# GRU step of a fused Trainium2 kernel: reset and update gate products laid into one strip of 128 PSUM columns

## What is computed

```python
def cell(h, x):
    gi = x @ W_ih + b_ih
    gh = h @ W_hh + b_hh
    i_r, i_z, i_n = jnp.split(gi, 3, axis=-1)
    h_r, h_z, h_n = jnp.split(gh, 3, axis=-1)
    r = jax.nn.sigmoid(i_r + h_r)
    z = jax.nn.sigmoid(i_z + h_z)
    n = jnp.tanh(i_n + r * h_n)
    h_new = (1.0 - z) * n + z * h
    return (h_new, h_new)
```

## Time and profile before

| | |
|---|---|
| median of 3 runs | 1900.22 us |
| lowest, highest | 1894.44, 1901.37 us |
| span of the profiled execution | 1898.4 us |
| PE, PEld, DVE, ACT, POOL busy | 91%, 61%, 68%, 41%, 16% |
| mean granted clock of PE | 0.992 of full speed |
| matmuls and weight loads | 41087 each |

### The profile page before, as it was taken

One profiled execution on the slowest core, in us unless ns is written; L12 is line 12 of the kernel. 1 busy time (PEld: TensorE's weight loads), 2 busy tenths in 40 slices (PEclk: granted clock), 3 DMA queues, 4 the chain that ended last, 5 costly groups with the idle time before them and its releaser, 6 DMA issues.

```text
span 1898.4 us, 95651 instructions
## 1 busy us (share of the span) xinstructions
PE 1724.2 (91%) x41087; PEld 1165.7 (61%) x41087; DVE 1297.8 (68%) x5788; ACT 779.8 (41%) x2714; POOL 300.4 (16%) x600
## 2 busy tenths in 40 slices
PE   6888888878889999989899999989799999988998
PEld 5777677666556666656566666656566666664444
DVE  6888778887667777767676767667677777764323
ACT  5655566543234343423234444432234444323442
POOL 2222222221211110121211111121211111121001
PEclk8999999999999999999999999999999999999999
DMA  7435444444326667425336677426336666439994
GB/s 259 142 144 195 172 166 170 153 187 137 125 89 193 197 209 220 147 86 147 118 89 196 197 215 212 146 72 169 102 104 203 192 202 192 135 91 372 389 357 147
DMA packets 176689, 334.06 MB, mean 176 GB/s; under 512 B 46448, under 2 KB 46600, under 8 KB 176264
## 3 DMA queue, kind: packets, MB, share of 16 engines
q1 hardware_dynamic: 171144, 311.17, 51.1%
q0 software_dynamic: 5120, 16.78, 2.7%
HBM read 263.10 MB, written 64.78 MB: 173 GB/s over the span
## 4 chain that ended last, share of the span: by engine, by line
PE 66%; DVE 16%; ACT 6%; issue 5%; SPq 3%; DMA 2%; another core or an unknown queue 1%; DVEq 0%; POOL 0%; ACTq 0%
PE bank_g L681 15%; PE bank L967 14%; PE bank_g L686 12%; PE bank_g L697 9%; PE bank L987 7%; DVE xt L1439 5%; DVE na L1445 3%; DVE pre L1441 3%; DVE hs_early L1451 3%; ACT seq_h L1113 3%; ACT rz L1113 3%; PE bank L723 2%; PE bank L963 1%; PE bank L949 1%; PE bank_l L973 1%
## 5 line engine op out<-in xcount | busy, mean ns | idle before, releaser
L1841 POOL COPY hxs<-hs 128x32 f16<-128x32 f16 x512 | 223.8, 437 | 1380.8 <-DVE hs L1459 1380.8
L681 PE MATMUL bank_g<-whh,hs_early 128*32 128x256 f16 x8192 | 319.0, 276 | 123.1 <-DVE hs_early L1451 122.1
L1113 ACT ACTIVATE rz<-pre 128x32 f32<-128x32 f32 x512 | 125.9, 246 | 737.2 <-DVE pre L1441 736.3
L1439 DVE STREAM_TRANSPOSE xt<-bank_g 128x256 f32<-128x256 f32 x512 | 231.0, 451 | 212.8 <-PE bank_g L686 198.8
L681 PEld LDWEIGHTS bank_g<-whh,hs_early 128*32 128x32 f16 x8192 | 171.4, 96 | 318.5 <-DVE hs_early L1451 312.9
L697 PE MATMUL bank_g<-whh,hs 128*32 128x128 f16 x16384 | 327.9, 220 | 10.9 <-issue 10.5
L686 PE MATMUL bank_g<-whh,hs 128*32 128x256 f16 x8192 | 314.6, 274 | 0.1
L967 PE MATMUL bank<-wm,wih 128*128 128x512 f16 x1272 | 309.7, 381 | 3.1 <-issue 2.4
L697 PEld LDWEIGHTS bank_g<-whh,hs 128*32 128x32 f16 x16384 | 259.8, 97 | 15.3 <-issue 12.5
L686 PEld LDWEIGHTS bank_g<-whh,hs 128*32 128x32 f16 x8192 | 204.5, 96 | 22.8 <-DVE hs L1459 3.4
L1113 ACT ACTIVATE seq_h<-na 128x16 f32<-128x16 f32 x512 | 114.9, 224 | 237.5 <-DVE na L1445 237.5
(11 more groups left out here) (245 smaller groups left out, 2063.0 us busy)
## 6 DMA issues: line engine op xcount, KB each, us to landing
wm<-moe_split SPq DMA_DIRECT2D x318, 512.0 KB, 4.5
wm<-in_w_moe SPq DMA_DIRECT2D x32, 768.0 KB, 5.4
moe_split<-wm SPq DMA_DIRECT2D x32, 768.0 KB, 5.1
wih<-x_rows SPq DMA_DIRECT2D x58, 256.0 KB, 4.7
y_rows<-wih SPq DMA_DIRECT2D x58, 256.0 KB, 4.6
whh<-moe_split SPq DMA_DIRECT2D x24, 512.0 KB
gi<-moe_split SPq DMA_DIRECT2D x18, 512.0 KB, 6.6
xr<-in_x SPq DMA_DIRECT2D x16, 512.0 KB, 4.1
```

The source lines that it names most:

```text
L681: mm(out_strip(0, j, 2 * P), early_cols[:, 8 * B * k:8 * B * (k + 1)], strip(whh[:, 1, k, 0:2 * D], j), start=(k == 0), stop=False)
L1113: return nc.scalar.activation(dst, src, func, **kw)
L1439: link(V.transpose(rows, bank_g[0][:, 0:2 * P].rearrange("p (m c) -> p m c", c=32)))
L1841: Q.tensor_copy(hxs[:, par, :, :, :, col].rearrange("p s k b -> p s (k b)"), hs_new).then_inc(S["h_kept"], 1)
```

## The change

The columns of z are no longer laid beside those of r. The state's tile is read two columns further left for z, so that the same state stands in columns 6 and 7 of a group instead of 4 and 5, and z's product comes out in rows 6 and 7 of the same 128 columns that hold r in rows 4 and 5. Two sets (`SETS`), r and z, so share one strip: each matmul has 128 columns, there are twice as many of them, each with its own weight load, and the bank's used part is half as wide. One transposition of 128 columns serves both. The tiles `hs` and `hs_early` get one more group of zeros in front, since z's first piece reads two columns ahead of the first group. `xt` and `pre` are laid out to match, and the access patterns of the input's copy, the reduce and the sigmoid change, with as many elements as before. The n gate is as it was.

```diff
--- before.py
+++ after.py
@@ -32,6 +32,12 @@
 
 
 GROUP = 3
+
+
+
+SETS = 2
+CHUNKS = 2 * K // SETS
+SET_COLS = 2 * D // SETS
 AS, WS = 16.0, 64.0
 PS = AS * WS
 
@@ -219,13 +225,13 @@
         bi = sb("bi", [P, G3], F32)
         bh = sb("bh", [P, G3], F32)
         hh = sb("hh", [P, K * B, 2], F32)
-        hs = sb("hs", [P, K * B, 8], F16)
-        hs_early = sb("hs_early", [P, K * B, 8], F16)
-        xt = sb("xt", [P, 2 * K, 64], F32)
+        hs = sb("hs", [P, 1 + K * B, 8], F16)
+        hs_early = sb("hs_early", [P, 1 + K * B, 8], F16)
+        xt = sb("xt", [P, CHUNKS, 64], F32)
         bias_to = sb("bias_to", [P, 8 * B], F16)
         bias_n = sb("bias_n", [P, D], F16)
         xt_n = sb("xt_n", [P, 4, K * B, GROUP], F32)
-        pre = sb("pre", [P, 2 * K, B], F32)
+        pre = sb("pre", [P, CHUNKS, B, SETS], F32)
         rz = sb("rz", [P, 2 * K * B, GROUP], F32)
         na = sb("na", [P, K * B, GROUP], F32)
         omz = sb("omz", [P, K * B, 2], F32)
@@ -342,16 +348,18 @@
         p_gw = bank_l[1][:, 2 * P:2 * P + B * K * E].rearrange("p (b k e) -> p b k e", b=B, k=K)
         h = hh[:, :, 1:2].rearrange("p (k b) o -> p k (b o)", b=B)
         hs_cols, early_cols = (v[:, :, :].rearrange("p g i -> p (g i)") for v in (hs, hs_early))
-        hs_new = hs[:, :, :].rearrange("p g i -> p i g")[:, 4:6]
+        hs_new = hs[:, 1:].rearrange("p g i -> p i g")[:, 4:6]
         hs_hi, hs_lo = hs_new[:, 0], hs_new[:, 1]
-        early_scan = early_cols.rearrange("p (c s) -> p s c", s=4)[:, 0]
-        early_hi = hs_early[:, :, 4]
-        ext = xt[:, :, 9:16 * B:16]
-        rows = xt[:, :, :].rearrange("p m (c o) -> p m c o", o=2)[:, :, :, 0]
-        terms = xt[:, :, :].rearrange("p m (b i) -> p m b i", i=16)[:, :, :, 8:11]
+        early_scan = early_cols[:, 8:].rearrange("p (c s) -> p s c", s=4)[:, 0]
+        early_hi = hs_early[:, 1:, 4]
+        ext = xt[:, :, :].rearrange("p g (b q i) -> p q g b i", b=B, i=4)[:, SETS:, :, :, 1]
+        rows = xt[:, :, :].rearrange("p g (c o) -> p g c o", o=2)[:, :, :, 0]
+        terms = xt[:, :, :].rearrange("p g (b q i) -> p (g b) q i", b=B, i=4)[:, :, SETS:, 0:3]
         rows_n = xt_n[:, :, :, 0:2].rearrange("p q g s -> p g q s")
         seq_n = xt_n[:, 2]
-        r_new, z_new, n_new = rz[:, :, GROUP - 1:GROUP], rz[:, K * B:, GROUP - 1:GROUP], na[:, :, GROUP - 1:GROUP]
+        pre_sets = pre[:, :, :, :].rearrange("p g b q -> p q (g b)")
+        rz_new = rz[:, :, GROUP - 1:GROUP].rearrange("p (q g) o -> p q (g o)", q=SETS)
+        z_new, n_new = rz[:, K * B:, GROUP - 1:GROUP], na[:, :, GROUP - 1:GROUP]
         pairs = {n: v[:, :, :].rearrange("p a o -> p (a o)") for n, v in
                  (("r", rz[:, 0:K * B]), ("seq_n", seq_n), ("na", na), ("omz", omz), ("seq_h", seq_h), ("hh", hh))}
 
@@ -395,6 +403,14 @@
         def strip(v, j):
 
             return v.rearrange("p (g j c) -> p j g c", j=K, c=32)[:, j]
+
+        def state(v, k, q):
+
+            return v[:, 8 + 8 * B * k - 2 * q:8 + 8 * B * (k + 1) - 2 * q]
+
+        def of_set(w, k, q):
+
+            return whh[:, w, k, q * SET_COLS:(q + 1) * SET_COLS]
 
         def out_strip(i, j, n):
 
@@ -677,14 +693,16 @@
 
                 pe.wait_ge(S["h_hi"], t + 1)
                 for k in range(K):
-                    for j in range(K):
-                        mm(out_strip(0, j, 2 * P), early_cols[:, 8 * B * k:8 * B * (k + 1)],
-                           strip(whh[:, 1, k, 0:2 * D], j), start=(k == 0), stop=False)
+                    for q in range(SETS):
+                        for j in range(K):
+                            mm(out_strip(0, j, SET_COLS // 4), state(early_cols, k, q), strip(of_set(1, k, q), j),
+                               start=(k == 0 and q == 0), stop=False)
                 pe.wait_ge(S["h_ready"], t + 1)
                 for k in range(K):
-                    for j in range(K):
-                        i = mm(out_strip(0, j, 2 * P), hs_cols[:, 8 * B * k:8 * B * (k + 1)],
-                               strip(whh[:, 0, k, 0:2 * D], j), start=False, stop=(k == K - 1))
+                    for q in range(SETS):
+                        for j in range(K):
+                            i = mm(out_strip(0, j, SET_COLS // 4), state(hs_cols, k, q), strip(of_set(0, k, q), j),
+                                   start=False, stop=(k == K - 1 and q == SETS - 1))
                 i.then_inc(S["gates_mm"], 1)
                 if t == 0:
                     pe.wait_ge(S["bias_row"], 1)
@@ -694,7 +712,7 @@
                 for k in range(K):
                     for w in range(2):
                         for j in range(K):
-                            i = mm(out_strip(1, j, P), hs_cols[:, 8 * B * k:8 * B * (k + 1)],
+                            i = mm(out_strip(1, j, P), state(hs_cols, k, 0),
                                    strip(whh[:, w, k, 2 * D:], j), start=False, stop=(k == K - 1 and w == 1))
                 i.then_inc(S["gates_mm"], 1)
 
@@ -1116,14 +1134,13 @@
 
                 act.wait_ge(S["n_pre"], t)
                 now = gi[:, col // TB, :, :, col % TB:col % TB + 1]
-                run(ext.unsqueeze(3), now[:, 0:2 * K], ACT.Copy)
+                run(ext, now[:, 0:2 * K, :, 0].rearrange("p (q g) b -> p q g b", q=SETS), ACT.Copy)
                 run(seq_n[:, :, GROUP - 1:GROUP].rearrange("p (k b) o -> p k b o", b=B), now[:, 2 * K:], ACT.Copy
                     ).then_inc(S["now_in"], 1)
 
             def gru_rz(t):
                 act.wait_ge(S["rz_pre"], t + 1)
-                run(r_new.rearrange("p a o -> p (a o)"), pre[:, :, :].rearrange("p m b -> p (m b)"),
-                    ACT.Sigmoid, scale=1 / PS).then_inc(S["rz_done"], 1)
+                run(rz_new, pre_sets, ACT.Sigmoid, scale=1 / PS).then_inc(S["rz_done"], 1)
 
             def gru_n(t):
                 act.wait_ge(S["n_pre"], t + 1)
@@ -1436,9 +1453,10 @@
                     dve.wait_ge(S["gru_chain"], t * GRU_CHAIN + n[0])
 
                 dve.wait_ge(S["gates_mm"], t * 2 + 1)
-                link(V.transpose(rows, bank_g[0][:, 0:2 * P].rearrange("p (m c) -> p m c", c=32)))
+                link(V.transpose(rows, bank_g[0][:, 0:SET_COLS // 4].rearrange("p (g c) -> p g c", c=32)))
                 dve.wait_ge(S["now_in"], t + 1)
-                V.tensor_reduce(pre[:, :, :], terms, AX, ALU.add).then_inc(S["rz_pre"], 1)
+                V.tensor_reduce(pre[:, :, :, :].rearrange("p g b q -> p (g b) q"), terms, AX, ALU.add
+                                ).then_inc(S["rz_pre"], 1)
                 dve.wait_ge(S["gates_mm"], t * 2 + 2)
                 link(V.transpose(rows_n, bank_g[1][:, 0:P].rearrange("p (g q s) -> p g q s", q=4, s=2)))
                 dve.wait_ge(S["rz_done"], t + 1)
```

## The result

The changed kernel takes 2163.66 us (median of 4 runs, 2152.71 to 2169.81) against 1900.8 us before (4 runs): 1.1395 times as long, with a 95% interval of 1.1354 to 1.1435. The forecast was 1980, its range ended at 2045. The direction and the main cause were as forecast; the loss is 263 us instead of 80.

The account below looks back on a forecast made before the run. The prediction took each GRU step as bound by its 3.13 us loop and PE's list of work: 1900.2 us, less 23 for the shorter loop, plus 103 net for code-fetch stalls, gives 1980; range 1915 to 2045.

Parts of the forecast that it names:

- loop shorter, and stalls that hide in spare time: GRU steps: shorter loop gains 23 us; some 11 us of stalls hide in PE's spare time in the first stretch.
- stalls, less those that were there: PE's chunk borders: 122 us of stalls from late code fetches, less the 8 us already in the run.
- half clock after stalls: PE's clock during or after stalls: the prediction had no such term.
- The loop: GRU step's chain: transposition saves 0.135 us, split product costs 0.022, so 0.113 us shorter where PE has spare time.
- the 14.3 of the sum: First 128 steps: all have the spare time for the shorter loop, a gain of 14.3 us before code stalls.
- The reading of the code stream: PE's instruction fetch: chunks of 256 instructions, two held, the next requested on entering the present; 438 chunks.
- The chunk's duration: PE's 256 instructions last 3.4 us in 74% of positions, some 4.1 us on average else.
- The size of the stall term: Chunk borders: fetches exceed chunk durations by 0.33 or 0.13 us on average; over 438 chunks, 122 us of stalls.
- the bound of 0.3 us: Code fetches: if packets queue behind a denser stream and take 0.3 us longer, 175 us gross, +160 net.
- The hidden fetch: Rival: code is requested early enough, so only the shorter loop's 23 us gain is left: 1877 us; chance 0.13.
- the two that end near zero: Rivals: stalls of 15 to 33 us cancel the gain (1891 to 1910), or dearer slot products (1893); chance 0.08.
- The test that the prediction made on the kernel before: Stall count applied to the kernel before: 310 x 0.04 = 12 us where 8 are seen, so right to a third.

Follow-up runs that it names:

- experiment 1: Kernel before with only its r/z product cut into twice as many matmuls of 128 columns, layout and transposition of 256 kept: 2175.3 us.
- 2: Kernel before with only the late half of its r/z product cut into matmuls of 128 columns, the first product left whole: 1988.06 us.
- 4: Changed kernel with the n product halved (no low half of W_hh), 16 matmuls and 16 weight loads fewer a step, no wait moved: 1961.71 us.
- 5: Changed kernel without the early r/z product and without PE's wait for h_hi, so one wait a step: 1837.24 us.
- experiment 3: Changed kernel without the early r/z product, 32 matmuls and weight loads fewer a step, leaving two PE waits in a row: 1975.98 us.
- experiment 7: Changed kernel with three quarters of the expert weights' columns not loaded in the slots, first two tiles excepted: 1998.58 us, against 2128.09 unchanged.
- 6: Kernel before with one more, already fulfilled, PE wait ahead of each step's first weight load: 1946.09 us.
- experiment 10: Changed kernel run again as it is, on a chip where the kernel before takes 1859.62 us: 2128.09 us.
- experiment 8: Kernel before with VectorE's waits for ACT's results (sigmoid, tanh) written first, ahead of those on its own chain: 1829.42 us against 1859.29.

## Why the prediction was right in kind and wrong in size

The spans differ by 269.6 us, and the 511 steps' intervals account for 270.2 of them. By the steps' records:

| | forecast, us | measured, us |
|---|---|---|
| loop shorter, and stalls that hide in spare time | -23 - 11 = -34 | -35 |
| stalls, less those that were there | 122 - 8 = 114 | 276.6 - 12.8 = 264 |
| half clock after stalls | none | 41 |
| sum | 80 | 270 |

The third row is read from the 44 steps that touch a half clock: they last 88.0 us longer than those of before, their stalls are 46.7 of it. The first row is what is left of the other 467 steps: 182.3 us longer, with 229.9 us of stalls, against before's 12.8. It is a remainder, so that it comes within 1 us of the forecast says less than it seems.

*The loop.* Right. 3.020 us a step in the first stretch (forecast 3.02), 3.127 in the slots (3.12 to 3.13), the transposition 319 ns (316), the product's cost on the loop 0.020 us by experiment 1 (0.02). In the first 128 steps the mean went from 3.189 to 3.748 us, 71.6 in all, while stalls rose by 85.8: the rest is -14.2. That this looks like the 14.3 of the sum is chance: the forecast had another 11 us there, of stalls hidden in spare time, and some 5 us of the rest are half clock. Gain and hidden stalls together are thus about 19 us in this stretch, where 25 were forecast.

*The reading of the code stream.* Right in mechanism: chunks of 256 instructions, one chunk ahead, 438 of them, stalls in hundreds at their borders. Experiments 1, 2 and 4 tie the stalls to the count of instructions, and 1 and 5 clear the rest of the change; experiment 3 shows that the count is not all. The Trainium skill, "Advanced Engine Details and Errata", section "ISA Cache", gives lines of 256 instructions and two of them. The spacing of the stalls, 256, agrees, and so does that in the kernel after no packet starts more than 0.11 us before the chunk ahead of it is entered; nothing here shows more than these two, though the same list gives TensorE 128 KB.

*The chunk's duration.* Right: 3.4 us without its stall was forecast for three of four, the median is 3.39.

*The size of the stall term.* This is the step that failed. The prediction took a fetch as 0.65, 0.86, 1.6 and 2.4 us to the packet's start, plus 2.3, from the kernel before, and got a mean excess of 0.33 us over 3.4 and of 0.13 over 4.1. In the kernel after the start is 1.09, 1.34, 2.05 and 2.96, and from start to use 2.42: the excesses are 0.69 and 0.31, and 438 x (0.74 x 0.69 + 0.26 x 0.31) = 259 us, near the 277 seen. These starts are read from the run itself, so this forecasts nothing, but it shows that the form of the sum held and its input did not. A fetch became 0.6 us longer at the median; the bound of 0.3 us, taken for a denser stream, was too small by half. Two parts of it can be seen. Packets wait in the DMA engines' traffic: with 67 GB/s in the slots instead of 148, 104 us of stalls went away (experiment 7). And a fetch that follows a stalled chunk starts later: median 1.46 us against 1.15 after a chunk without a stall, as it would if a stall made the next one likelier. This second part is a correlation in the records and was not tried by itself. The stretch from 137.92 shows that with nearly idle DMA engines, too, a stalled chunk took 4.00 us, against the 3.15 us that I had as a median fetch. Using the distribution of a kernel that hardly stalls for one that does was the error.

*The clock.* This term was put at nothing, without a reason given, and it is the second part of what failed. 41 us of the loss lie in steps at half clock, beyond their stalls. It was not tried by an experiment of its own, and a quarter of the windows follow a wait and not a stall.

*The range.* It left a few per cent beyond 2045 us, and the time came out 119 us beyond. Both wrong terms err to the same side.

*The rivals.* The hidden fetch is out, and with it the two that end near zero, with 277 us of stalls. The Trainium skill ("Runtime: NRT & Kernel Launch", section "Instruction fetch mechanics") has a crossing "mostly hidden"; here 282 of 438 crossings show a stall, 0.98 us on average. The test that the prediction made on the kernel before (12 us where 8, or by these records 12.8, were seen) could not catch the error, for it was made where chunks last 5.5 us and hardly any fetch matters.

*What stays open.* Why packets start so late in experiment 3 (half of them after 2.76 us, with no more instructions than before). The lone wait before the product is needed for it, as 5 shows, but not enough, as 6 shows.

## What to carry to other kernels

Where PE runs small matmuls at a few nanoseconds an instruction, count its instructions between waits as a resource: a chunk of 256 that is consumed faster than the next is fetched, here 3.5 to 4 us with packets in quiet DMA queues and more in busy ones, turns each shorter loop into a longer stall. Read the latency of a fetch from a stretch that already stalls, not from one that never needed it, and look whether the clock falls with the stalls. Before trading instructions for a shorter loop, look whether the same loop has a wait that stands alone: its order cost nothing and gave what this change was after.

## What the runs showed of the hardware that was not expected

- The duration of a stalled chunk, from first instruction to first instruction, is not spread evenly: it clusters at 3.47, 3.74, 4.01, 4.29, 4.56, 4.84, 5.11 and 5.39 us, 0.274 apart. Of the 282 in after 143 lie within 0.02 us of that grid, where an even spread would put 42; in experiment 10 they are 156 of 289. In experiment 3 the grid does not show: 24 of some 180, no more than an even spread puts there. What steps by 0.274 us is not known.
- A fulfilled wait that stands alone costs PE 0.086 us a step at the head of the product (experiment 6) and VectorE 0.057 each (experiment 8, two of them, 0.114 a step).
- PE went to its half clock around stalls of 2.7 and 3.3 us, and 32 matmuls side by side in four strips then took 1.07 us instead of 0.62. The mean clock is 0.966 in after, 0.972 in experiment 1, 0.983 in 2 and 0.992 in before. But it is 0.971, 0.973 and 0.978 in experiments 3 to 5, which leave matmuls out and stall less than 1, so stalls are not all that lowers it.
